# Mamba preparation in two other PSUM banks, emptied behind the exponentials, its plan shifted, and filler products at two norms

## The reference

```python
h = layernorm(x) * (1 + ca) + sa;  x = x + ga * attention_block(h)      # group norm, linear attention with decay,
                                                                        # second group norm, small SiLU network
h = layernorm(x) * (1 + cb) + sb;  x = x + gb * experts(h)              # 8 experts of 512 hidden units, the best 2 count
h = layernorm(x) * (1 + ca) + sa;  x = x + ga * mamba(h)                # below
h = layernorm(x) * (1 + cb) + sb;  x = x + gb * sparse_fft_filter(h)

# mamba(h): 256 inner channels, 16 states
xv, z = split(h @ W_in.T);  xv = silu(causal_conv4(xv) + conv_b)
dt = softplus(h[:, :64] @ W_dt.T + b_dt);  B = h @ W_B.T;  C = h @ W_C.T
s[t] = exp(dt[t] * A) * s[t-1] + (dt[t] * xv[t]) * B[t];  y[t] = sum_n s[t, n] * C[t, n]
return (y * silu(z)) @ W_out.T
```

## Time and profile before

| what | value |
|---|---|
| median of 3 runs | 641.6 us (638.91 to 644.28) |
| profiled execution, its time | 644.56 us |
| profiled execution, its span (first to last instruction) | 642.3 us |
| busy, share of the span: PE, DVE, ACT, POOL | 78%, 67%, 57%, 58% |
| experts alone, 168.2 to 291.2 us: PE, DVE, ACT, POOL | 112.86, 35.27, 71.29, 15.25 us |
| experts beside the scan, 291.2 to 498.7 us: PE, DVE, ACT, POOL | 171.74, 164.09, 175.92, 180.61 us |
| scan alone, 498.7 to 620.8 us: PE, DVE, ACT, POOL | 87.86, 112.89, 60.83, 81.36 us |
| mean granted TensorE clock | 0.92 of 2.4 GHz |

### The profile page before, as it was taken

The page is one execution under the profiler, slowest core; times in us unless marked ns, Lnnn a source line. Parts: engine busy times, 40 slices in busy tenths (PEclk is TensorE's granted clock), DMA queues, the critical chain, the costliest instruction groups (busy, mean ns, idle before and its releaser), DMA issues.

```text
span 642.3 us, 6868 instructions
## 1 busy us (share of the span) xinstructions
PE 500.5 (78%) x2336; PEld 347.1 (54%) x2336; DVE 429.1 (67%) x723; ACT 368.4 (57%) x510; POOL 373.6 (58%) x234
## 2 busy tenths in 40 slices
PE   3568887659989889998887897877897867767663
PEld 3256555334667777756765566665566533333222
DVE  4667698953532324108997686996686997889971
ACT  0433242325654463769998888778888737744301
POOL 3125876747201011204999987899987778547651
PEclk9688798978989899999999898998898989978996
DMA  8500000000000000211110010120110112112100
GB/s 308 224 1 0 0 2 1 1 0 0 1 0 2 2 1 0 90 45 31 36 66 35 34 66 35 33 83 36 37 62 33 65 51 67 65 35 72 42 0 16
DMA packets 12561, 26.91 MB, mean 42 GB/s; under 512 B 1968, under 2 KB 7472, under 8 KB 12272
## 3 DMA queue, kind: packets, MB, share of 16 engines
q1 hardware_dynamic: 11952, 25.57, 11.5%
q10 hardware_dynamic: 576, 0.92, 0.4%
HBM read 25.31 MB, written 1.18 MB: 41 GB/s over the span
## 4 chain that ended last, share of the span: by engine, by line
PE 36%; DVE 28%; ACT 20%; issue 8%; POOL 7%; DMA 1%; ACTq 0%; POOLq 0%; DVEq 0%
DVE Hs L743 8%; PE pO L1204 7%; ACT gel L955 5%; DVE S L638 5%; DVE pCT L730 5%; PE pH L1242 5%; ACT dA L967 4%; PE pH L1192 3%; ACT L967 3%; DVE pH L637 3%; PE pH L1194 2%; PE pH L1193 2%; PE pY L1284 2%; POOL Zev L389 2%; POOL Zod L383 2%
## 5 line engine op out<-in xcount | busy, mean ns | idle before, releaser
L1204 PEld LDWEIGHTS pO<-w_e,gel 128*128 128x128 f32 x1024 | 126.4, 198 | 14.1 <-DVE X L714 6.9
L1204 PE MATMUL pO<-w_e,gel 128*128 128x128 f32 x1024 | 128.4, 282 | 5.2 <-DVE X L714 5.1
L743 DVE TENSOR_TENSOR_SCAN Hs<-dA,HL,pCT 128x512 f32<-128x512 f32 x96 | 117.7, 1267 | 13.5 <-ACT dA L967 5.6
L955 ACT ACTIVATE gel<-pH,b_e 128x512 f32<-128x512 f32 x128 | 86.1, 687 | 58.1 <-PE pH L1194 57.4
L967 ACT ACTIVATE dA<-dt,a_neg 128x512 f32<-128x512 f32 x128 | 81.8, 711 | 26.7 <-DVE Hs L743 26.4
L383 POOL TENSOR_TENSOR Zod<-Hs,Crow 128x1024 f32<-128x1024 f32 x33 | 79.8, 2419 | 18.7 <-DVE Hs L743 17.0
L730 DVE TENSOR_TENSOR pCT<-u,pB 128x1024 f32<-128x1024 f32 x64 | 78.3, 1224 | 18.4 <-PE pB L1267 17.4
L389 POOL TENSOR_TENSOR Zev<-Zev,Zod 128x1024 f32<-128x1024 f32 x33 | 78.2, 2369 | 2.6
L1192 PE MATMUL pH<-h2h,w_e1h 128*128 128x512 f32 x128 | 57.9, 453 | 25.2 <-ACT gel L955 23.3
L714 DVE SCALAR_TENSOR_TENSOR X<-pO,wts,X 128x128 f32<-128x128 f32 x128 | 35.8, 342 | 48.7 <-PE pO L1204 48.7
L383 POOL TENSOR_TENSOR Zev<-Hs,Crow 128x1024 f32<-128x1024 f32 x17 | 40.1, 2358 | 43.1 <-DVE Hs L743 39.7
(11 more groups left out here) (196 smaller groups left out, 932.0 us busy)
## 6 DMA issues: line engine op xcount, KB each, us to landing
Crow<-c_rows SPq DMA_DIRECT2D x32, 512.0 KB, 3.7
w_e<-in_w_e SPq DMA_DIRECT2D x2, 2048.0 KB, 10.7
X<-in_x SPq DMA_DIRECT2D x4, 256.0 KB, 7.1
out<-h2T SPq DMA_DIRECT2D x4, 256.0 KB, 2.9
S<-in_w_mod ACTq DMA_DIRECT2D x2, 384.0 KB, 5.2
w_cx<-in_conv_row SPq DMA_DIRECT2D x1, 512.0 KB, 8.9
w_f<-in_w_f SPq DMA_DIRECT2D x2, 128.0 KB, 5.8
b_e<-in_b_e SPq DMA_DIRECT2D x1, 256.0 KB, 13.3
```

The lines of the kernel that those rows point to most:

```text
L743: vec.tensor_tensor_scan(Hs[:, 2 * o + d, 0:w], dA[:, 4 * (p % 2) + 2 * o + d, 0:w], pU[:, d, 0:w], HL[:, d, n:n + 1] if c else 0.0, ALU.m ...
L955: nc.scalar.activation(gel[:, n % NG, 0:w], pH[n % 2][:, 0:w], ACT.Gelu_apprx_tanh, bias=b_e1[:, NK * e + k:NK * e + k + 1]).then_inc(s["m ...
L1204: ins = mm(pO[:, j * P:(j + 1) * P], gel[:, n % NG, j * P:(j + 1) * P], w_e2[:, NK * (g % E) + k, :], start=(k == 0 and j == 0), stop=(k = ...
```

## The change

`PS = [pH0, pH1, pY0, pY1]`, and a stage at place A of a pair before 18 now uses `pY0`, at B `pY1` (elsewhere `pY0`); from pair 18 on A is `pH0` and B `pH1` as before (`stage_bank`). This goes for all stages of the table, those of the experts too. On TensorE the B stages of a pair with an expert step stand behind half of the down products and the B row, not ahead of them. On ScalarE the decays of the next pair come ahead of the evacuations of A and B. The plan for the next chunk's preparation is another: x first, then rows and dt, z in the chunk's last pair, both parts, none left for the next chunk's first pair; `step` stands between the halves of the last pair and no longer at its end. Before the first totals TensorE waits until both banks have been read. And `warm` puts 11 products of `ident` and `X`, whose results nobody reads, around the two group norms.

```diff
+        PS = pH + pY
+        def stage_bank(p, at):
+            return (2 if p < ALONE else 0) + int(at == "B")
...
-                             (5, "A", "rows", front), (5, "B", "dt_part", front, 0), (6, "A", "dt_part", front, 1),
-                             (6, "B", "x_part", front, 0), (7, "A", "x_part", front, 1), (7, "B", "z_part", front, 0),
-                             (7, "end", "step", front)]
-                if 0 <= c < NL:
-                    plan += [(0, "A", "z_part", c, 1)]
+                             (5, "A", "x_part", front, 0), (5, "B", "rows", front), (6, "A", "x_part", front, 1),
+                             (6, "B", "dt_part", front, 0), (6, "C", "dt_part", front, 1), (7, "mid", "step", front),
+                             (7, "A", "z_part", front, 0), (7, "B", "z_part", front, 1)]
...
@@ ScalarE
                     hidden(p + AHEAD, range(NK))
-                run(stages, "AB")
-                if p is not None and 0 <= p + 1 < NL * NP:
+                if 0 <= p + 1 < NL * NP:
                     decays(p + 1)
-                run(stages, ("apply",))
-                run(stages, "C")
+                run(p, stages, "AB")
+                run(p, stages, ("apply",))
+                run(p, stages, "C")
...
@@ TensorE
+            def warm(bank, n):
+                for _ in range(n):
+                    mm(bank[:, :], ident[:, :], X[:, 0:NJ, :], start=True, stop=True)
+            warm(pH0, 2)
             pe.wait_ge(s["set_dve"], 2)
             gn(0)
+            warm(pH0, 3)
...
             out_part(NR * NC - 1)
+            warm(pB, 3)
             gn(1)
+            warm(pB, 3)
...
-                run(stages, "A")
-                if p > 0:
+                run(p, stages, "A")
+                if 0 < p < NL * NP:
                     total(p - 1)
-                run(stages, "B")
+                if not moe:
+                    run(p, stages, "B")
                 if moe:
                     down(g, 0)
                     down(g, 1)
                 if 0 <= 2 * p + 2 < NL * NS:
                     row_b(2 * p + 2)
                 if moe:
+                    run(p, stages, "B")
+                if moe:
                     down(g, 2)
                     down(g, 3)
-                run(stages, "C")
+                run(p, stages, "C")
...
+                if p == ALONE:
+                    use(2, "mam_y", 1)
+                    use(3, "mam_y", 1)
```

More of the change, by code:

```diff
@@ L491, in _ @@
             for p, stages in later_stages():
-                if p is not None and p >= 0:
+                if 0 <= p < NL * NP:
                     output(p, 0)
@@ L779, in _ @@
             for p, stages in later_stages():
-                g = p + AHEAD if p is not None else -1
-                scan = p is not None and p >= 0
+                g = p + AHEAD
+                scan = 0 <= p < NL * NP
                 if scan:
@@ L786, in _ @@
                     moe_acc(g - 1)
-                run(stages, False)
+                run(p, stages, False)
                 if scan:
@@ L790, in _ @@
                     scans(2 * p + 1)
-                run(stages, True)
+                run(p, stages, True)
         @block.scalar
@@ L1307, in _, with run @@
                     "rows": rows, "dt_part": dt_part, "z_part": z_part, "total": total, "project": project, "fft": fft}
-            def run(stages, places):
+            def run(p, stages, places):
                 for at, stage, *k in stages:
                     if at in places and stage in mine:
-                        mine[stage](*k, int(at != "A"))
+                        mine[stage](*k, stage_bank(p, at))
             for p, stages in later_stages():
-                if p is not None:
-                    pair(p, stages)
-                else:
-                    run(stages, "ABC")
+                pair(p, stages)
 def constants():
```

60 lines of the change are left out of this document (30 added, 30 removed).

## The result

The changed kernel takes 622.04 us, the median of four runs (618.62 to 623.89), beside 641.44 (638.91 to 644.28) for the kernel before. The ratio is 0.967 with a 95% interval of 0.963 to 0.971, so it is 3.3% faster. Run again on a later occasion it took 619.18 beside 643.03, ratio 0.962 (0.958 to 0.966). The forecast was 620, in a range of 612 to 632.

A forecast was written before the change was run, and what follows sets the result against it. TensorE was taken to bound the experts alone, GpSimd experts with scan, VectorE the scan alone. Terms 3.7 + 12.0 + 0 + 4.4 + 1.2 = 21.3 us off the median 641.6 gave 620, range 612 to 632.

The forecast's parts named there:

- The norms, -3.7: Fillers around both group norms keep TensorE's clock up: 1.7 us gained at norm 0, 2.0 at norm 1.
- The experts alone, -12.0: Before the scan, router behind half the down products: 3.25 us saved each, 9.75 in all, plus 1.9 and 0.4.
- the step after: Expert step following a router's: waits of 0.46 and 0.17 us go, 0.63 by three, 1.9 in all.
- Preparation of chunk 0, 0: Last three steps ahead of the scan: same products in another order, no gain, bounds -2 to +1.5 us.
- Preparation under the scan, -4.4: Chunks 1 and 2: GpSimd's gaps of 2.29 and 2.11 us at the chunk's start go; the second gaps stay.
- The new order fits under GpSimd: Pairs 5 to 7: preparation fits with nothing to spare; GpSimd's row operation still ready 3 to 4 us early.
- the sums that I called level: Work in pairs 5 to 7: TensorE 33.7 us, ScalarE about 34, GpSimd 34.1.
- ring: Rival, chance 0.05: exponentials, bank emptying and B rows wait on each other in preparing pairs; 46 us lost, 666.
- The scan alone, -1.2: After the experts: VectorE's 5.45 us of exponential waits go, but it waits about 2.1 us twice for B rows.
- The base: Starting time for the subtraction: median 641.6 us, 3 lower than the profiled 644.56.
- the change brings little: Rival, chance 0.05: the experts' gaps come back elsewhere, only 1.9 + 4.4 + 1.2 us remain, 634.
- preparation doesn't fit: Rival under GpSimd, chance 0.15: one late operation per chunk, 3 to 4 us, no chunk-start gain; 625 to 631.

The follow-up runs named there:

- the two router kernels: Changed kernel with the router's products ahead of the down products again, 632.42 us; the same with two filler products in the router's wait, 624.75 us.
- the late projection: Changed kernel with the previous chunk's projection one place later in a chunk's first pair, its row statistics behind it: 611.15 us, ratio 0.950.
- both edits: The late projection plus, in pairs 21 and 22, the B row and the second place's products ahead of the totals: 610.27 us, ratio 0.949.
- the early B row: Changed kernel with the B row right behind the x part in pairs 21 and 22: 619.47 us; in both edits 610.27; with two more fillers there 607.64.

## Why the prediction was right, and where it was off

- **The norms, -3.7: the mechanism right, one size off.** Norm 0 was put at 1.7 and its column gives 1.7. Norm 1 was put at 2.0 and gives 1.2. What is off is the part put as "the next two products also leave the slow clock". In the first two traces they did (5.75 us between the first expert products less 3.72 up to the last attention scan is 2.03), but equal kernels differ by 1 us in that column (34.05 and 35.11), and over all profiles 1.2 is left. Of these 2.9 us the runs show only 0.4 +- 2.6 in the time.
- **The experts alone, -12.0: right, with its parts.** The experts' column gained 13.6 in the first two traces, 13.3 of it in the six steps shown above. Wait and clock were put at 1.54 and 1.71 per router, the step after at 0.63; the two router kernels give 1.79, 1.64 and 0.75. The order of the cause is right too: the place does it, and the banks add 4.5 us for the experts' column. Of these 4.5 us 2.3 stand in two steps, the first and -4, which the kernel before does in 6.94 and 7.15 us too: there the banks only keep away what the new places would cost without them.
- **Preparation of chunk 0, 0: right.** The last three steps ahead of the scan and pair 0 take 43.7 us before (9.12 + 11.42 + 12.93 + 10.24) and 43.3 after (11.07 + 13.17 + 10.71 + 8.31). From the first Gelu of step -3 to the first scan it is 31.0 and 30.9.
- **Preparation under the scan, -4.4: right, a little small.** Both gaps at a chunk's head went, and the one behind the first gate shrank by 0.8; 5.5 us in all by GpSimd's starts. Putting the old table back brought both gaps back and 3.8 us by the same starts. The gaps of 4 to 5 us stayed for the reason given, as the late projection shows by removing them.
- **The new order fits under GpSimd: right.** It never waited for its row operation between 285 and 473 us by more than 0.32. But the sums that I called level hid how much rests on one line: with the exponentials behind the evacuations the same plan costs 30 us. The "ring" did not form. The kernel with the exponentials last comes near what I priced for it, 46 us, by a related way: TensorE waits for ScalarE with work for VectorE behind it. I had no rival for that order, because the change has the other.
- **The scan alone, -1.2: 1.3 in the third stretch (122.1 to 120.8), in the first profile by two errors that cancel.** The exponential waits went as said. The waits for B rows were 3.61 and 1.94 instead of 2.1 twice, since the first x part came at half clock. The projection of chunk 2 then ran at full clock (1.95 us, 3.62 before) and gave back 1.7, by no step of mine. In the second profile neither happened: the waits are 1.94 twice, 3.9 in all where I had 4.2, and the projection takes 3.38. From GpSimd's product behind the second gate to the end, before takes 140.9 us, the two profiles of the changed kernel 139.7 and 139.2. So the term holds there by its own steps, with 1.7 us. The 1.6 us that the second profile was expected to gain in this stretch came in chunk 2, and chunk 3 lost 1.2 of it.
- **The base.** Subtracting from 641.6 was right to within its spread: ten runs of the changed kernel have a median of 619.7. That the forecast lies so close is in part luck. The terms as measured in the profiles are 2.9 + 13.3 + 0.4 + 5.5 + 1.3 = 23.4 us, 2.1 more than the 21.3 forecast, and the two occasions gave 19.4 and 23.9 between the medians. The experts alone ended 19.3 us earlier, not 15 to 16: 2.6 of it is the attention column and 1.6 the experts' own column beyond its term.
- **Slips in the working, without effect on the 620.** Half of the down products takes 1.84 us by its starts (198.58 to 200.42), not 1.75, and GpSimd's sum for pairs 5 to 7 is 33.8, not 34.1. The rival "the change brings little" leaves out the fillers' 3.7 without a reason; with them it gives 630, not 634. The rival "preparation doesn't fit" adds 620 + 4.4 + 7 - 4, which is 627 and not 625 to 631, and the 4 has no source.

The Trainium skill (ScalarE: Activation LUTs, What ACT_TABLE_LOAD costs) would have made ScalarE the bound in the preparing pairs by its drain of 1.38 us. The traces agree with the rows of before instead: in the rows of exponentials last, the load starts at 334.65, takes 1.28, and the exponentials start at 335.95.

## What to carry to other kernels

A product that needs another engine's result belongs behind enough independent work to cover that engine's time; here that saved the wait and, as much again, the clock behind it. When such a product moves later, look at what the engine that empties its bank does next: that queue has to move too, or it passes the delay on. Where one engine bounds a stage, put the work that feeds it ahead of every wait that does not, and check a plan of places in each stage apart, because a table that is right beside experts was wrong without them.

## What the runs showed of the hardware that I had not expected

The same instructions behind the same gap can get either clock. TensorE's timeline at the second pair of chunk 0, late projection alone and then both edits (which differ only from pair 21 on):

```profile
277.31 0.39 PE L1282 MATMUL pB<-ST,sel 96*128 96x512 bf16 x1
279.61 0.50 PE L1204 MATMUL pH<-h2h,w_e1h 128*128 128x512 f32 x1 [1.91 <-ACT gel L958]
...
279.60:282.80 3.20, 3.19 (x22) 1.00 0.00 0
```
```profile
277.18 0.39 PE L1286 MATMUL pB<-ST,sel 96*128 96x512 bf16 x1
279.48 0.74 PE L1204 MATMUL pH<-h2h,w_e1h 128*128 128x512 f32 x1 [1.91 <-ACT gel L958]
...
279.50:282.70 3.20, 3.20 (x9) 0.51 0.00 0
```

Behind the same idle 1.91 us one run has granted clock 1.00 (2.4 GHz) and the other 0.51 (1.2 GHz), and the next B row starts at 284.33 instead of 282.88, 1.5 us later. The Trainium skill (TensorE: Matmul & The Clock Gate, What's actually happening) says that the phase of the gate differs from run to run; these traces agree that one gap gives one or the other. But the fall may not be mere chance here: the three profiles with the early B row have it behind this gap, though their program is the same up to pair 21, and the two of the changed kernel, the two without fillers and the late projection alone don't. Why is not shown. Ten runs of the changed kernel range over 8.6 us (615.3 to 623.9); how much of that such falls make is not shown either. An edit worth less than about 3 us can be seen in its own rows here, but not in a handful of times.
